# Convolution stage: VectorE's two-tile sums read PSUM, residual and channel exchange move to TensorE

## The reference, cut to what matters

```python
enh = conv_depthwise_3x3(conv_1x1(x))
h = conv_grouped_3x3(x)                      # 16 channels
h1, h2 = split(h, 2)
attn = conv_1x1(h1 * h2) * attgamma + conv_1x1(x)          # 16 coefficients for each pixel
attk = einsum('bpn,nm->bpm', attn, selfw)    # for each pixel and group a 2 x (2 * 9) kernel
y = einsum('bpgij,bpgj->bpgi', attk, patches(enh)) + attn @ selfb
out = y * ga1 + enh + x
```

## Time and profile before

| | us |
|---|---|
| Median of three timed runs (6273.13 to 6277.56) | 6275.48 |
| Profiled execution | 6276.51 |
| Its span, first to last instruction | 6274.8 |
| PE busy | 5891.0 (94%) |
| VectorE busy | 5583.1 (89%) |
| GpSimd busy | 4717.8 (75%) |
| ScalarE busy | 3479.6 (55%) |

### The profile page before, as it was taken

The page is one execution under the profiler, slowest core; times in us unless marked ns, Lnnn a source line. Parts: engine busy times, 40 slices in busy tenths (PEclk is TensorE's granted clock), DMA queues, the critical chain, the costliest instruction groups (busy, mean ns, idle before and its releaser), DMA issues.

```text
span 6274.8 us, 117188 instructions
## 1 busy us (share of the span) xinstructions
PE 5891.0 (94%) x39944; PEld 4198.9 (67%) x39944; DVE 5583.1 (89%) x5380; ACT 3479.6 (55%) x4284; POOL 4717.8 (75%) x1893
## 2 busy tenths in 40 slices
PE   8999999999977999999999999999999999999998
PEld 7888888888854666666666666665666666666666
DVE  7888888888868989999988999998998998899999
ACT  6888888888854444444444444444444444444443
POOL 4665555555548888888888888888888888888886
PEclk9999999999988999999999999999999999999999
DMA  2222222222221212212112112121211212122121
GB/s 88 74 74 74 74 74 74 75 77 76 74 59 56 63 59 64 63 61 64 62 60 64 61 61 64 60 63 59 64 62 59 67 59 62 57 64 64 60 64 44
DMA packets 303718, 408.06 MB, mean 65 GB/s; under 512 B 38192, under 2 KB 202736, under 8 KB 303344
## 3 DMA queue, kind: packets, MB, share of 16 engines
q1 hardware_dynamic: 303008, 402.45, 20.1%
q10 hardware_dynamic: 400, 0.69, 0.1%
HBM read 152.26 MB, written 136.31 MB: 46 GB/s over the span
## 4 chain that ended last, share of the span: by engine, by line
PE 54%; DVE 9%; issue 7%; SPq 1%; POOL 0%; DVEq 0%; DMA 0%; ACT 0%; POOLq 0%
PE ps_k L862 18%; PE ps_t L878 18%; PE ps_m L845 10%; DVE products L1091 6%; PE ps_p L831 4%; DVE products L1098 2%; PE ps_t L895 2%; PE ps_t L886 1%; PE ps_t L893 1%; PE ps_m L852 0%; DVE h_prod L1115 0%; DVE products L1057 0%; SPq L667 0%; POOL enh L789 0%; SPq L717 0%
## 5 line engine op out<-in xcount | busy, mean ns | idle before, releaser
L1091 DVE TENSOR_TENSOR products<-ps_k,enh 128x1024 f32<-128x1024 f32 x2304 | 2754.8, 1218 | 401.0 <-PE ps_k L862 380.5
L789 POOL TENSOR_TENSOR enh<-enh,tap 128x1280 f32<-128x1280 f32 (+1 forms) x1024 | 2845.1, 2778 | 149.2 <-ACT tap L1008 97.9
L862 PE MATMUL ps_k<-att,basis 128*128 128x512 f32 x4608 | 1778.6, 469 | 229.0 <-DVE products L1091 189.8
L878 PE MATMUL ps_t<-ident,products 128*128 128x128 f32 x12288 | 1608.0, 277 | 65.4 <-DVE products L1091 45.5
L878 PEld LDWEIGHTS ps_t<-ident,products 128*128 128x128 f32 x12288 | 1460.3, 143 | 257.8 <-issue 78.4
L862 PEld LDWEIGHTS ps_k<-att,basis 128*128 128x128 f32 x4608 | 726.8, 191 | 1121.9 <-DVE products L1091 638.4
L1008 ACT ACTIVATE tap<-e,dw 128x1280 f32<-128x1280 f32 (+1 forms) x1024 | 1245.8, 1248 | 7.6 <-POOL enh L789 7.6
L280 POOL TENSOR_TENSOR hidden_lo<-hidden,hidden_hi 128x1024 fp32r<-128x1024 f32 x256 | 692.8, 2725 | 717.9 <-DVE hidden_hi L485 717.9
L1098 DVE TENSOR_TENSOR products<-products 128x1024 f32<-128x1024 f32 x512 | 1064.7, 2080 | 0.0
L801 POOL TENSOR_TENSOR products<-products 128x1024 f32<-128x1024 f32 x256 | 613.8, 2398 | 415.4 <-DVE products L1091 415.4
L845 PE MATMUL ps_m<-xin,gT 128*32 128x512 f32 x4608 | 822.5, 617 | 9.6 <-DVE bias_att L1048 9.6
(11 more groups left out here) (106 smaller groups left out, 7000.9 us busy)
## 6 DMA issues: line engine op xcount, KB each, us to landing
xt<-in_x SPq DMA_DIRECT2D x128, 512.0 KB, 4.0
layer_out<-xo SPq DMA_DIRECT2D x128, 512.0 KB, 2.9
out<-out_sb SPq DMA_DIRECT2D x256, 256.0 KB, 2.0
xin<-layer_out SPq DMA_DIRECT2D x63, 896.0 KB, 6.0
enh<-enh SPq DMA_DIRECT2D x128, 325.0 KB, 3.1
enh<-enh SPq DMA_DIRECT2D x128, 260.0 KB, 2.4
xin<-layer_out SPq DMA_DIRECT2D x63, 384.0 KB, 7.3
att<-att_hi SPq DMA_DIRECT2D x512, 32.0 KB, 1.9
```

What stands on the lines that cost most here:

```text
L789: nc.gpsimd.tensor_tensor(own, own, tap_sb[add % TAP_BUFFERS][:, 0:hi - lo, :], ALU.add).then_inc(dw_done, 1)
L862: mm = nc.tensor.matmul(ps_k[q % 2][:, BANK * s:BANK * (s + 1)], basis[:, 2 * t + s, :], att[p][:, j, :], start=True, stop=True)
L878: mm = nc.tensor.matmul(ps_t[j % 2][:, C * r:C * (r + 1)], products[:, q % PRODUCTS, s, C * r:C * (r + 1)], ident[:, :], is_transpose=True ...
L1091: nc.vector.tensor_tensor(products[:, q % PRODUCTS, :, :].rearrange("c s (h w) -> c s h w", w=W), ps_k[q % 2][:, :].rearrange("c (s h w) - ...
```

## The change

It has five parts, all in `convolve`.

1. Merges. For q in VECTOR_MERGES the product is written back into its own PSUM banks, the next product goes to SBUF, and the merge right behind it adds the PSUM operand to it. The list OPS so has the merge one product earlier. KERNEL_BUFFER and KERNEL_FREE give each kernel pair the buffer that is freed next: an in-place product frees none, its merge does.
2. Channel exchange. enh has one copy; the product takes it twice (a broadcast operand). The basis columns are swapped for s = 1, and PE transposes that half of each term with ident_swap, a permuted identity, as the moving tile. The swap DMAs go.
3. Residual. enh comes in through the basis: own_row adds 1 to the kernel of the centre tap, own channel (ones are put into a spare row of att). x comes from DRAM a second time into x_own, half a band each, and is transposed where enh_x was. Both enh_x additions go.
4. h_prod is taken from PSUM with the bias in one operation. xin is one DMA instead of two.
5. A step now has 44 slots, one for each VectorE operation. All tables of places are new: terms, back, convolution, 1x1, taps, GpSimd's merges. products has 14 places.

```diff
-PRODUCTS = 12
+PRODUCTS = 14
...
-OPS = [op for q in range(Q) for op in [("product", q)] + [("merge", q - 2)] * (q - 2 in VECTOR_MERGES)]
+OPS = [op for q in range(Q) for op in [("product", q)] + [("merge", q - 1)] * (q - 1 in VECTOR_MERGES)]
...
+FREEING = [(OP_COUNT[op], op[1]) for op in OPS if op[0] == "merge" or op[1] not in VECTOR_MERGES]
+KERNEL_BUFFER = {0: 0, 1: 1}
+for q in range(2, Q):
+    KERNEL_BUFFER[q] = KERNEL_BUFFER[FREEING[q - 2][1]]
+assert [KERNEL_BUFFER[q] for _, q in FREEING[-2:]] == [0, 1]
+KERNEL_FREE = {q: FREEING[q - 2][0] if q >= 2 else FREEING[q - 2][0] - SLOTS_IN_BAND for q in range(Q)}
+KERNEL_SLOT = {q: KERNEL_FREE[q] - 1 for q in range(Q)}
...
+STORED = [q for q in range(Q) if q not in VECTOR_MERGES]
+PLACE = {q: i % PRODUCTS for i, q in enumerate(STORED)}
...
-TERM_SLOT = dict(zip(TERMS, (3, 4, 8, 9, 13, 11, 11, 16, 18, 19, 21, 19, 22, 24, 25, 26, 30, 28, 31, 33, 35, 36, 40, 37)))
+TERM_SLOT = {1: 4, 2: 5, 4: 11, 5: 9, 6: 15, 8: 12, 9: 13, 11: 18, 13: 19, 14: 20, 15: 26, 17: 23, 19: 26, 20: 27, 22: 34, 23: 33, 24: 35, 26: 36, 28: 37, 29: 39, 31: 41, 32: 42, 33: 48, 35: 45}
...
-BACK_SLOTS = [15, 23, 32, 42]
+BACK_SLOTS = [21, 30, 38, 54]
...
-CONV_SLOTS = [28, 28, 29, 31, 34, 34, 37, 37, 38, 39, 42, 43, 43, 46, 46, 48, 48, 50]
...
+POOL_MERGE_PLACES = (2.1, 4.5, 10.5, 13.45)
...
+CONV_SLOTS = [33, 33, 40, 40, 43, 43, 43, 43, 50, 50, 52, 52, 56, 56, 59, 59, 62, 62]
+COEFFICIENT_SLOT = 28
+PW_SLOTS = [17, 22, 24, 29, 31]
...
-        enh = [sb(f"enh{p}", [C, 2, EROWS, WP]) for p in range(2)]
-        enh_x = sb("enh_x", [C, ROWS, W])
+        enh = [sb(f"enh{p}", [C, EROWS, WP]) for p in range(2)]
+        x_own = [sb(f"x_own{h}", [C, ROWS // 2, W]) for h in range(2)]
...
-                def swap_channels(m, p, h):
-
-                    sp.wait_ge(enh_ready, 2 * m + h + 1)
-                    lo, hi = HALVES[h]
-                    for i in range(2):
-                        sp.dma_start(enh[p][i:C:2, 1, lo:hi, :], enh[p][1 - i:C:2, 0, lo:hi, :]).then_inc(swapped[p][h], 16)
-
                 def loads(m, p):
-
-                    for i, (lo, hi) in enumerate(((0, ADD_SPLIT + 2), (ADD_SPLIT + 2, XROWS))):
-                        at_least(sp, enh_x_ready[i], m - 1)
-                        sp.dma_start(xin[p][:, lo:hi, 1:W + 1], x_band(m, lo, hi)).then_inc(x_in[p], 16)
+                    at_least(sp, pw_done, PW_CHUNKS * (m - 1))
+                    at_least(sp, conv_done, m - 1)
+                    sp.dma_start(xin[p][:, :, 1:W + 1], x_band(m, 0, XROWS)).then_inc(x_in[p], 16)
+
+                def load_own(n, h):
+                    lo = ROWS // 2 * h
+                    at_least(sp, sum_done, CHUNKS * (n - 1) + 2 * h + 2)
+                    sp.dma_start(x_own[h][:, :, :], x_band(n, PAD + lo, PAD + lo + ROWS // 2)).then_inc(own_in[h], 16)
...
-                        swap_channels(n, p, 1)
+                        load_own(n, 0)
...
-                def add_input(n, p):
-                    pool.wait_ge(dw_done, 2 * (TAPS - 1) * (n + 1))
-                    at_least(pool, sum_done, CHUNKS * n)
-                    nc.gpsimd.tensor_tensor(enh_x[:, 0:ADD_SPLIT, :], enh[p][:, 0, 1:ADD_SPLIT + 1, 1:W + 1],
-                                            xin[p][:, 2:ADD_SPLIT + 2, 1:W + 1], ALU.add).then_inc(enh_x_ready[0], 1)
...
-                    if q >= 2:
-                        pe.wait_ge(product_ready, len(OPS) * n + OP_COUNT["product", q - 2])
-                    else:
-                        at_least(pe, product_ready, len(OPS) * (n - 1) + OP_COUNT["product", q + Q - 2])
+                    at_least(pe, product_ready, SLOTS_IN_BAND * n + KERNEL_FREE[q])
                     for s in range(2):
-                        mm = nc.tensor.matmul(ps_k[q % 2][:, BANK * s:BANK * (s + 1)], basis[:, 2 * t + s, :], att[p][:, j, :],
-                                              start=True, stop=True)
+                        mm = nc.tensor.matmul(ps_k[KERNEL_BUFFER[q]][:, BANK * s:BANK * (s + 1)], basis[:, 2 * t + s, :],
+                                              att[p][:, j, :], start=True, stop=True)
...
-                    for s in range(2):
+                    for s, turn in enumerate((ident, ident_swap)):
                         for r in range(CHUNK_ROWS):
-                            mm = nc.tensor.matmul(ps_t[j % 2][:, C * r:C * (r + 1)], products[:, q % PRODUCTS, s, C * r:C * (r + 1)],
-                                                  ident[:, :], is_transpose=True, start=(q == FIRST_TERM[j] and s == 0 and r == 0),
+                            mm = nc.tensor.matmul(ps_t[j % 2][:, C * r:C * (r + 1)], products[:, PLACE[q], s, C * r:C * (r + 1)],
+                                                  turn[:, :], is_transpose=True, start=(q == FIRST_TERM[j] and s == 0 and r == 0),
...
-                        if CHUNK_ROWS * j in (0, ADD_SPLIT):
-                            pe.wait_ge(enh_x_ready[j > 0], n + 1)
+                        if j % 2 == 0:
+                            pe.wait_ge(own_in[j // 2], 16 * n + 16)
                         for r in range(CHUNK_ROWS):
-                            mm = nc.tensor.matmul(ps_t[j % 2][:, C * r:C * (r + 1)], enh_x[:, CHUNK_ROWS * j + r, :], ident[:, :],
+                            mm = nc.tensor.matmul(ps_t[j % 2][:, C * r:C * (r + 1)], x_own[j // 2][:, CHUNK_ROWS * (j % 2) + r, :], ident[:, :],
...
+                for i in range(2):
+                    nc.vector.tensor_copy(ident_swap[:, :].rearrange("k (g i) -> k g i", i=2)[:, :, i:i + 1],
+                                          ident[:, :].rearrange("k (g i) -> k g i", i=2)[:, :, 1 - i:2 - i]).then_inc(swap_ready, 1)
...
+                own = basis_full[:, 2 * (TAPS // 2), :]
+                nc.vector.tensor_scalar(own, own, own_row[:, 0:1], None, ALU.add).then_inc(setup_step, 1)
...
-                    nc.vector.tensor_tensor(products[:, q % PRODUCTS, :, :].rearrange("c s (h w) -> c s h w", w=W),
-                                            ps_k[q % 2][:, :].rearrange("c (s h w) -> c s h w", s=2, w=W),
-                                            enh[p][:, :, r:r + CHUNK_ROWS, dx:dx + W], ALU.mult).then_inc(product_ready, 1)
+                    kernels = ps_k[KERNEL_BUFFER[q]][:, :].rearrange("c (s h w) -> c s h w", s=2, w=W)
+                    if q in VECTOR_MERGES:
+                        out = kernels
+                    else:
+                        place_free(n, q)
+                        out = products[:, PLACE[q], :, :].rearrange("c s (h w) -> c s h w", w=W)
+                    nc.vector.tensor_tensor(out, kernels, enh[p][:, r:r + CHUNK_ROWS, dx:dx + W].unsqueeze(1).to_broadcast([C, 2, CHUNK_ROWS, W]),
+                                            ALU.mult).then_inc(product_ready, 1)
...
-                    lead = products[:, q % PRODUCTS, :, :]
-                    nc.vector.tensor_tensor(lead, lead, products[:, (q + 1) % PRODUCTS, :, :], ALU.add).then_inc(product_ready, 1)
+                    dve.wait_ge(product_ready, SLOTS_IN_BAND * n + OP_COUNT["product", q + 1])
+                    both = products[:, PLACE[q + 1], :, :].rearrange("c s w -> c (s w)")
+                    nc.vector.tensor_tensor(both, ps_k[KERNEL_BUFFER[q]][:, :], both, ALU.add).then_inc(product_ready, 1)
...
+                                dve.wait_ge(moved, 64 * (m + 1))
+                                dve.wait_ge(conv_done, m + 1)
+                                nc.vector.scalar_tensor_tensor(out=h_prod[:, :], in0=ps_m[:, :], scalar=bias_h[:, 0:1], in1=h_up[:, :],
+                                                               op0=ALU.add, op1=ALU.mult).then_inc(h_prod_ready, 1)
...
```

More of the change, by code:

```diff
@@ L582, in sem @@
             return ctx.enter_context(nc.semaphore(name))
-        ident = sb("ident2", [C, C])
+        ident, ident_swap = sb("ident2", [C, C]), sb("ident_swap", [C, C])
+        own_row = sb("own_row", [C, 1])
         pw_raw = sb("pw_raw", [C, C])
@@ L732, in step @@
                         loads(l, p)
+                    if n is not None:
+                        load_own(n, 1)
                     if m is not None:
@@ L905, in step @@
                                 pointwise(l, p, c)
-                    for q in range(Q):
-                        if n is not None and q + 2 < Q:
-                            basis_kernels(n, p, q + 2)
-                        elif m is not None and q + 2 >= Q:
-                            if q + 2 == Q and isinstance(m, int) and m == 0:
-                                pe.wait_ge(basis_ready, 2)
-                            if q + 2 == Q:
-                                pe.wait_ge(att_in[b], rounds(m, b, 256) + 256)
-                            basis_kernels(m, b, q + 2 - Q)
-                        for band, parity, slot in ((o, b, q + Q), (n, p, q)):
+                    for at in range(SLOTS_IN_BAND):
+                        for band, parity, slot in ((n, p, at), (m, b, at - SLOTS_IN_BAND)):
```

(19 more changed lines are left out.)

130 lines of the change are left out of this document (59 added, 71 removed).

## The result

| | before | after |
|---|---|---|
| Median | 6275.32 (6273.13 to 6277.56) | 5733.09 (5726.21 to 5734.46, four runs) |
| Profiled execution, its span | 6276.51, 6274.8 | 5731.75, 5730.0 |
| Mean granted TensorE clock | 0.981 | 0.993 |

The ratio is 0.9134 [0.9118, 0.915]. The forecast was 5937 us, its range 5855 to 6070: the sign and the bound (PE) were right, the size was not.

What follows compares the result with a forecast made beforehand. PE was taken as the bound after the change: 60.3 us work + 1.6 turn + 0.4 kernel waits + 0.6 late input = 62.9 us a band, 5.3 less; over 64 bands 339 us off 6276.5, so 5937 us, range 5855 to 6070.

Steps and rivals of the forecast that it cites:

- the sign: Whole kernel: the change makes it faster, chance 0.93; within 0.02, slower 0.05.
- (a): PE at the loop's turn, once in two bands: its idle time stays, 1.6 us a band.
- Rival 3: Convolution bands: input in time, no stall but the turn, 5873 us; part of the turn covered too, 5840; chance 0.12.
- PE work: PE's busy time per band: 63.6 us falls by 3.3, from regrouped convolution matmuls and fewer places, to 60.3 us.
- xin late: First pointwise matmul waits for the single input DMA: 0.3 to 1.0 us a band, taken as 0.6.
- VectorE busy: VectorE per band: shorter merges, residual addition moved to PE, h_prod from PSUM; 61.8 us falls by 9.1 to 52.7.
- The coupling term: Kernel pairs on PE wait for their slot's VectorE operation: 0.4 us a band, possibly 0 to 3.
- the lower bound: VectorE's product written back into PSUM: takes as long as the ordinary product, 1.22 us; above, 2.4 us.
- rival 4: In-place PSUM product takes 2.4 us and delays PE: up to 6545 us; chance still faster 0.03, no change 0.01, slower 0.04.
- rival 1: Input load: the single transfer takes 1.5 us more beside other traffic, band 64.4 us, 6033 us; chance 0.13.
- GpSimd hidden: GpSimd per band: 54 us at most beside 62; its four sums finish several us before their terms.
- The mechanism of the long merges: VectorE merges: reading two SBUF tiles beside busy GpSimd makes them long; one from PSUM saves 7.0 us a band over eight.

Runs made afterwards that it cites:

- b_shift: Kernel before with 256 satisfied waits (128 idle instructions) on PE ahead of the convolution loop, loop unchanged: 6122.98 us, against 6274.55 beside it.
- experiment one: Changed kernel with its grouped convolution matmuls spread again, six places of four and six of two instead of nine of four: 5960.85 us, 228 more.
- experiment three: Changed kernel with SP's load of xin issued ahead of the last chunk's store instead of behind it: 5697.39 us, ratio to before 0.908.
- experiment two: Changed kernel with its eight merges reading both operands from SBUF, the PSUM product left out of the sum: 6054.52 us, 321 more.

## Why the prediction was wrong, point by point

**The step that failed** is (a): "The loop's turn: I keep 1.6 us; the loop holds two bands as before." I read the two idle times of the earlier trace rows as a property of the branch. They were a reload of PE's code, which depends on where the body lies, and the change moved it by 32 instructions. Measured at the turn: 0. A reload taken out of the kernel before gave 152 us, put into the changed one it cost 135, of the 204 that the forecast was off. Rival 3 had "if part of the turn is covered too, 5840", as an afterthought with no mechanism.

**What hung on it.** The turn cost more than its idle. The stretch behind a turn of the kernel before has clock 0.79 in the busy row of 3698 to 3706 us; PE had stood idle 1.50 us before 3698.6 and stood idle 2.16 us before 3701.5:

```profile
3698.00:3706.00 8.00, 5.24 (x28) 3.82 (x28) 5.83 (x3) 2.91 (x3) 7.76 (x4) 0.79 0.17 69
```

After the stall PE runs for a while at the lower of its two levels (1.2 instead of 2.4 GHz), and this was counted in my 63.6 us of PE work. It does so behind 28 of the 29 turns; the turn that I had read in the earlier trace rows is the one without it (clock 1.00 from 3564 to 3572 us), so those rows could not have shown it. Without the reload, at clock 1.00, the kernel before (b_shift) has 2864.19 / 3000 x 65.5 = 62.5 us. So 1.1 us of "work" was the turn's as well.

**The terms, per band:**

| | forecast | measured |
|---|---|---|
| PE work | 63.6 - 3.3 = 60.3 | 2966.40 / 3000 x 59.2 = 58.5 |
| turn | 1.6 | 0 |
| kernel pairs' waits | 0.4 | 2.2 / 33.8 = 0.07 |
| xin late | 0.6 | 20.4 / 33.8 = 0.60 |
| VectorE busy | 52.7 | 2724.77 / 3000 x 59.2 = 53.8 |

PE's work is 1.8 lower than forecast: 1.1 is the clock, 0.3 the regrouping, which gave 3.6 (experiment one) where I had 3.3, and 0.4 is not taken apart. The coupling term was mis-sized, 0.4 for 0.07. Outside the bands the time seems to grow: 6274.8 - 64 x 68.2 = 1910 us before, 5730.0 - 64 x 59.2 = 1941 after, where I had put less than 2 us. About half of these 31 us is in my count: 68.2 holds for the 58 bands of the 29 turns, and the six others never had the reload's 1.6 + 1.1 us, 16 us in all. The rest is open. Together 5937 - 64 x (1.6 + 1.1 + 0.7 + 0.33) + 31 = 5729; this closes by itself, since the 0.7 and the 31 are remainders.

**What held.** The merge at 1.22 us with no spread; the in-place product at 1.23 us, near the lower bound (rival 4 is out); h_prod at 0.74; the input 0.6 late, and 36 us in all (experiment three; rival 1 is out); VectorE 1.1 us above its 52.7, which cost nothing, since PE is the bound; GpSimd hidden. The mechanism of the long merges held too, and more sharply than I had it (experiment two). The rule of the Trainium skill (VectorE: DVE Perf Modes, the section on the TRN2 errata) that I had weighed against the change, an estimate of 65 ns more per merge from PSUM, is not borne out: 1225 ns median from PSUM and SBUF, where the shortest from two SBUF tiles was 1209, 16 ns.

**What the gain is made of.** The reload: 152 us where it was taken from the kernel before (6275 to 6123), 135 where it was put back into the changed one. The change gets this by luck: nothing in it aims at the place of the loop. The rest, 6123 - 5733 = 390 us, is the change proper. Of this, undoing the merges alone costs 321 and the regrouping alone 228; they are more than the 390 together, since the new order with both undone is slower than the old. One way through the runs, all single but the last: the regrouping in the old order loses 7 us (6123 to 6130), all other parts but the short merges gain 76 (6130 to 6055), the short merges 321 (6055 to 5733). The residual, the channel exchange and the new order were not tried singly.

## What to carry to other kernels

Where an engine stalls at every turn of a loop, look at the instruction queue's packets before taking the stall as given: if they come with each turn, the body may only lie badly, and a change ahead of it or in it can gain or lose that time, even one that adds instructions without work. Compare these packets in every pair of profiles before the difference is put down to an edit. An engine's busy time is work only at one clock: price a band at clock 1.00. What a saving on an engine is worth depends on the order around it: the same regrouping was worth 228 us and 243 us in the new order, with short merges and with long ones, and nothing in the old order, where PE's waits grew by what its work had lost.

## What the runs showed of the hardware that was not expected

- PE's loop of some 1650 instructions is either kept whole or loaded whole (9 packets of 16.4 KB a turn), by its place; 128 idle instructions ahead of the loop made the kernel 2.4% faster, 200 made the other 2.4% slower.
- In the kernel before, the stall of 3.3 us at the turn is followed by the lower clock, behind 28 of 29 turns; this costs 1.1 us a band beside the stall's 1.6. The lower clock needs no reload: with long merges in the new order and 30 packets the mean granted clock is 0.984, against 0.993 with short ones.
- VectorE writes a product back into the PSUM banks that it reads in 1232 ns, 7 more than into SBUF (medians).
- VectorE with two SBUF operands waits for GpSimd's addition under way and then takes 1.08 us more (157 of 158 merges of the kernel before). The two slow each other: a merge 1211 to 3642 ns (mean 1.87 us) against 1211 to 1227, a GpSimd addition of 1280 elements 3023 ns against 2704.
